# A fused decoder layer on one core: a third score bank, transforms folded in half, and shared-expert steps moved behind the last expert blocks

## The reference

```python
x = _layernorm(x + attn(x))        # 16 heads of 8, 4 key heads, rms norm and rope on q and k,
                                   # scores 50*tanh(s/50), causal softmax
x = _layernorm(x + xattn(x, ctx))  # cross attention to 32 context rows gives c_t; then
    x = layernorm(x_text) * (1 + mod_gate * scale_in) + mod_gate * shift_in      # scales from c_t
    Kf = jnp.fft.rfft(K, n=2 * L, axis=-1)             # K: kernel of a 64-state recurrence, 512 taps
    xf = jnp.fft.rfft(x, n=2 * L, axis=1)
    y = jnp.fft.irfft(xf * Kf.T[None], n=2 * L, axis=1)[:, :L] + x * D_skip
    xt = x_text + y * (1 + mod_gate * scale_out) + mod_gate * shift_out
    return layernorm(xt + gelu(layernorm(xt) @ W1 + b1) @ W2 + b2)
x = _layernorm(x + ffn(x))         # mean of 2 shared experts of width 512, plus the top 2 of 8
                                   # routed experts of width 512, weighted by a softmax of the gates
```

## Time and profile before

| | |
|---|---|
| median of 3 runs | 561.07 us (558.0 to 561.37) |
| profiled execution | 563.88 us, its span 562.1 us |
| granted TensorE clock, mean | 0.904 |
| PE busy | 443.5 us (79%) |
| DVE busy | 330.3 us (59%) |
| ACT busy | 328.2 us (58%) |
| POOL busy | 247.3 us (44%) |
| DMA | 51.53 MB, mean 92 GB/s |

### The profile page before, as it was taken

How to read it: one execution, slowest core, us unless ns; L and a number is a source line. 1 busy time by engine, 2 the same in 40 slices (tenths; PEclk the granted TensorE clock), 3 DMA queues, 4 the chain that set the end, 5 groups by cost and what they waited for, 6 DMA issues and landing times.

```text
span 562.1 us, 9639 instructions
## 1 busy us (share of the span) xinstructions
PE 443.5 (79%) x3343; PEld 316.1 (56%) x3361; DVE 330.3 (59%) x983; ACT 328.2 (58%) x567; POOL 247.3 (44%) x306
## 2 busy tenths in 40 slices
PE   4656667378988879788798999999979699989830
PEld 3322323145657633567346865787778666878830
DVE  7877968847876565866754775546245310334214
ACT  4279769997775888877896152215536343445410
POOL 3513264423561565614446244864283574044341
PEclk9856656679999999999999999999998899999985
DMA  3788300002101000000000200165485516769831
GB/s 94 267 181 152 100 2 1 0 2 58 77 1 77 20 2 0 2 1 1 2 0 1 76 2 19 40 179 194 138 260 160 163 54 182 261 208 279 271 104 37
DMA packets 39920, 51.53 MB, mean 92 GB/s; under 512 B 8769, under 2 KB 29025, under 8 KB 39873
## 3 DMA queue, kind: packets, MB, share of 16 engines
q1 hardware_dynamic: 37376, 45.78, 28.1%
q0 software_dynamic: 2496, 5.15, 2.6%
HBM read 41.25 MB, written 13.86 MB: 98 GB/s over the span
## 4 chain that ended last, share of the span: by engine, by line
PE 47%; ACT 22%; DVE 9%; issue 8%; POOL 8%; DMA 5%; another core or an unknown queue 1%; POOLq 0%; SPq 0%; ACTq 0%; DVEq 0%
ACT probs L1082 8%; PE ring_s L957 5%; ACT probs L1088 5%; PE bank_o L987 4%; PE bank_o L775 4%; PE bank_d L865 3%; DMA token_pairs<-y_blk,x_blk 3%; PE ring_s L760 3%; PE bank_o L973 3%; PE ring_s L951 3%; POOL expert_rows L1302 3%; PE ring_u L852 3%; PE bank_d L894 2%; PE ring_u L844 2%; PE bank_r L641 2%
## 5 line engine op out<-in xcount | busy, mean ns | idle before, releaser
L1082 ACT ACTIVATE probs<-ring_s 128x512 f32<-128x512 f32 (+1 forms) x192 | 92.3, 524 | 39.2 <-PE ring_s L760 19.5
L760 PE MATMUL ring_s<-qT,kT 128*128 128x128 bf16 (+3 forms) x238 | 62.5, 330 | 41.6 <-ACT probs L1082 31.3
L1254 POOL TENSOR_SCALAR_AFFINE_SELECT probs<-probs 128x256 f32<-128x256 f32 (+1 forms) x96 | 50.6, 558 | 100.1 <-ACT probs L1088 100.1
L1135 ACT ACTIVATE g_ring<-ring_s,w_blk 128x128 f32<-128x128 f32 x184 | 52.3, 371 | 47.5 <-PE ring_s L957 47.5
L1088 ACT ACTIVATE probs<-probs 128x2560 f32<-128x2560 f32 x32 | 74.4, 2335 | 1.1
L1311 POOL DMA_INDIRECT token_pairs<-y_blk,x_blk x46 | 44.6, 970 | 66.2 <-DVE y_blk L1838 59.9
L760 PEld LDWEIGHTS ring_s<-qT,kT 128*128 128x128 bf16 x256 | 20.8, 100 | 80.2 <-ACT probs L1082 61.0
L957 PE MATMUL ring_s<-xT_blk,w_blk 128*128 128x128 f32 x368 | 51.1, 284 | 5.9 <-DVE xT_blk L1831 3.9
L1188 POOL TENSOR_TENSOR rstd<-var_eps,neg_half 128x4 f32<-128x4 f32 x24 | 25.0, 1040 | 67.4 <-DVE var_eps L1507 67.4
L957 PEld LDWEIGHTS ring_s<-xT_blk,w_blk 128*128 128x128 f32 x368 | 46.5, 198 | 7.9 <-ACT g_ring L1135 4.3
L775 PE MATMUL bank_o<-probs,vv 128*32 128x128 f32 (+3 forms) x512 | 43.2, 483 | 3.7 <-POOL probs L1254 3.6
(11 more groups left out here) (365 smaller groups left out, 932.3 us busy)
## 6 DMA issues: line engine op xcount, KB each, us to landing
w_blk<-expert_pack SPq DMA_DIRECT2D x46, 514.0 KB, 5.0
expert_pack<-in_L_ffn_W SPq DMA_DIRECT2D x16, 256.0 KB, 8.9
expert_rows<-blank SPq DMA_DIRECT2D x6, 520.0 KB, 3.6
x_blk<-expert_rows SPq DMA_DIRECT2D x10, 260.0 KB, 4.4
y_pair<-token_pairs SPq DMA_DIRECT2D x4, 512.0 KB, 4.9
x_in<-in_x SPq DMA_DIRECT2D x4, 256.0 KB, 2.9
cosm<-in_c_cos SPq DMA_DIRECT2D x1, 1024.0 KB, 5.9
sin_fwd<-in_c_sin_fwd SPq DMA_DIRECT2D x1, 1024.0 KB, 8.8
```

The source lines that it names most:

```text
L760: last = mm(bank[:, c:c + w], kT[:, r, p // 2, P * j:P * (j + 1)], qT[:, p, P * j:SEQ], start=True, stop=True)
L1082: f(probs[:, pair % PAIRS_HELD, BASE[n]:BASE[n] + WIDTH[n]], ring_s[k % 2][:, 0:WIDTH[n]], ACT.Tanh, scale=1.0 / (CAP * float(np.sqrt(np.f ...
L1135: last = f(g_ring[:, s % RING, P * n:P * (n + 1)], ring_s[s % 2][:, P * n:P * (n + 1)], ACT.Gelu, bias=w_blk[:, k % SLOTS, HID + n:HID + n ...
L1254: last = g.affine_select(out=v, in_=v, compare_op=ALU.is_ge, fill=0.0, base=0, pattern=[[0, v.shape[1]], [1, P]], channel_multiplier=-1)
```

## The change

- **Score banks.** `ring_s` has three banks; the third is what was `bank_m`. A head pair takes five fills of 512 columns, since the last two of 256 share one. `rows`, `yT` and the vectors go to `bank_o`, and PV waits until the tokens of the PV before it have been read there. The block transposes use `ring_s[2]`.
- **Folded transforms.** Frequencies are sorted into even and odd, and samples into sums and differences with their mirror image, so that a step of `dft` or `conv` has two matmuls in place of four. New are `mirror` (two matmuls with a matrix that reverses rows), `fold` on DVE, `unfold` on DVE (three instructions) and `back` (two matmuls); `shape_out` is in two instructions. The kernel is transformed the same way (`kmirror`, `kfold`). The tables are half as wide and shifted by half a step, which DVE computes at the start (`halves`, some 25 instructions on 128x4, and four times `half`, four instructions on 128x256); the forward tables are made by 16 transposes (`tab`) and four copies on ACT. `spectra` has 17 instructions in place of 3.
- **Units.** The last six shared units of batch 3 come behind the last block, as units 72 to 77; group 1's blocks are 49 to 71. The downs of these blocks alternate between `bank_d` and `ring_u[0]`, so that the sum of batch 3 can stay in `bank_o`.
- **Buffers and SP.** Six `y_blk` in place of three, four slots of `g_ring` in place of three. SP issues a group's first six weight loads ahead of the wait for the scatters.
- **New lists** for all four engines.

```diff
-FILLS = [(r, tiles) for tiles in ([(0, 0)], [(1, 0), (3, 384)], [(2, 0)]) for r in range(2)]
+FILLS = [[(r, j, c) for j, c in tiles] for tiles in ([(0, 0)], [(1, 0), (3, 384)]) for r in range(2)] + [[(0, 2, 0), (1, 2, 256)]]
+BANKS = 3
-RING = 3
+RING = 4
-YS = 3
+YS = 6
+LATE = 6
+UNITS = shared_units(0) + shared_units(1) + block_units(0) + shared_units(2) + shared_units(3)[:-LATE] + block_units(1) + shared_units(3)[-LATE:]
 PE_ORDER = steps("""
-    xT.0 qkv.0 fold1 fold2 fold3 fold4 vectors qT.0.0 qT.0.1 qT.0.2 qT.0.3 qT.0.4 s.0.0.0 s.0.0.1 s.0.0.2 s.0.0.3
+    xT.0 qkv.0 fold1 fold2 fold3 fold4 vectors pack qT.0.0 qT.0.1 qT.0.2 qT.0.3 qT.0.4 qT.0.5 s.0.0.0 s.0.0.1 s.0.0.2
...
 ACT_ORDER = steps("""
-    xT.0 qkv.0 functions fold1 fold2 fold3 qT.0.0 qT.0.2 qT.0.4 s.0.0.0 s.0.0.1 s.0.0.2 s.0.0.3 s.0.0.4 s.0.0.5
+    functions xT.0 qkv.0 fold1 fold2 fold3 qT.0.0 qT.0.2 qT.0.4 s.0.0.0 s.0.0.1 s.0.0.2 s.0.0.3 s.0.0.4 s.0.1.0
...
+            def turn_over(dst, src, at):
+                for j in range(NJ):
+                    last = mm(dst[:, P * j:P * (j + 1)], flip[:, :], src[:, at + NJ - 1 - j, :], start=True, stop=True)
+                return last
+
+            def half_dft(f, c, src):
+                at = 0 if (f == 0) == (c < NJ) else NJ
+                for j in range(NJ):
+                    last = mm(ring_u[f][:, P * c:P * (c + 1)], (cos_fwd, sin_fwd)[f][:, j, P * c:P * (c + 1)], src[:, at + j, :],
+                              start=(j == 0), stop=(j == NJ - 1))
+                return last
...
             def values(quad):
                 b, q = divmod(quad, NQUAD)
                 pe.wait_ge(masked, 2 * quad + 2)
-                if quad >= 1:
-                    pe.wait_ge(oT_ready, quad)
+                if quad == 0:
+                    pe.wait_ge(b1_ready, 1)
+                else:
+                    pe.wait_ge(y_ready, quad)
...
+            def mirror(b):
+                pe.wait_ge(xmod_ready, b + 1)
+                turn_over(ring_u[0], xn, NJ).then_inc(mirror_ps, 1)
...
+            def back(b):
+                pe.wait_ge(unfolded, b + 1)
+                turn_over(bank_d, unrolled, NJ).then_inc(back_ps, 1)
...
+            def unfold(b):
+                dve.wait_ge(conv_ps, b + 1)
+                sym, anti = (bank_d[:, HALF * k:HALF * (k + 1)].rearrange("p (j d) -> p j d", j=NJ) for k in range(2))
+                one(v.tensor_copy(unrolled[:, 0:NJ, :], anti))
+                one(tt(unrolled[:, NJ:NT, :], sym, unrolled[:, 0:NJ, :], ALU.subtract))
+                tt(unrolled[:, 0:NJ, :], sym, unrolled[:, 0:NJ, :], ALU.add).then_inc(unfolded, 1)
...
             for g in range(GROUPS):
                 sp.wait_ge(table_ready, g + 1)
+                for q in range(SLOTS):
+                    load_block(g * NB + q)
+                if g:
+                    sent(g - 1)
+                    load_pair(GB * (g - 1))
                 sp.wait_ge(scattered[g], 16 * 2 * NT * GB)
```

488 lines of the change are left out of this document (285 added, 203 removed).

## The result

The changed kernel takes 552.5 us (median of 4 runs, 551.69 to 552.84) against 560.9 us before; the ratio is 0.9859, 95% interval 0.9829 to 0.9889. That is 8.4 us, where 30 were forecast. In the profiled executions the last norm ends at 545.22 us in place of 556.21, 11.0 us sooner (the profiled execution of before was 3 us above its median, that of after at its median). Every ratio here leaves out executions over 1.5% above the fastest of their kernel, while the medians hold all.

What follows compares the result with a forecast made beforehand. PE was taken to bound about 128 to 539 us, DVE the first 34, the tail its own chain. 562.1 + 11 - 24.9 - 3 + 6 - 6 - 6 + 4.3 - 11.5 = 532.0, against the median 531 us; range 512 to 554.

Steps and rivals of the forecast that it cites:

- Folded transforms, -24.9 and -3: PE's transforms: 28 fewer matmuls a batch save 24.9 us over four batches; the kernel's own transform saves about 3.
- The start, +11: Up to the first tanh: new ACT and DVE work delays it 17.3 us, partly given back in ACT's idle time; net +11.
- New waits, +6: In the batches' transforms: PE waits for DVE's fold, unfold and halved shape_out, costing 6 us (bounds 0 and 12).
- Third bank, -6: From 128 to 345 us: PE's 9.9 us of waits for ACT to leave a score bank shrink, saving 6 us.
- Buffers, -6: In the expert blocks: six y_blk and four gelu slots remove DVE's scatter waits and PE's idle time, saving 6 us.
- Readiness, +4.3: At both groups' starts: PE arrives before the rows are loaded, costing 3 us for group 0 and 1.3 for group 1.
- Tail, -11.5: After the last block's down: shared units run beside the closing chain, so down and end come 11.5 us sooner.
- B: Whole kernel: start +17, folding's waits 12, readiness 8 and ring -3 eat the savings; 550 us, chance 0.16.
- C: PE's clock falls behind the added exchanges, four falls of 2.5 us each; 541 us, chance 0.05.
- E: Up to 345 us DVE becomes the bound, folding there brings nothing, start stays +17; slower at 574 us, chance 0.06.

## Why the prediction was wrong

The sign and the range were right; the size was not (30 us forecast, 8.4 measured). Of the 21.6 us that are missing the table has 5.9 at the 16th exp, 10.1 between it and the first scatter, and 3.1 behind that (the rest is the profile of before against its median).

- **Folded transforms, -24.9 and -3: the step that failed.** It said that "all four lie where PE sets the pace: batches 0 to 2 in the 217 us at 88%". A busy share of 88% isn't a bound. In the old lists, where I had read that row, the halved matmuls gave 0.9 us of the 18.7 that lie there, at most about 6.5 with the clock held up (estimate), and the changed kernel as a whole gained 10.1 in that stretch where I had 20.2. What took the saving there were waits of PE for ACT, POOL and DVE (32.6 us idle in place of 22.3) and, behind them, the lower clock. Doubling the matmuls in the new lists cost in full, so a busy row can be a bound from one side only. How the 10.1 divides among folding, third bank and new lists stays open: no run has the new lists with one of them alone. Batch 3's share, behind the attention, is in the 16.7 us that PE's busy time fell there.
- **The start, +11: the give-back was the error.** Undoing order and tables gave back 13.6 us at the 16th exp. The first tanh was 13.6 late; I had 17.3 with 8.8 coming back in ACT's idle time. Nothing came back, and the tables took the place of what could have: DVE is the busiest engine up to 117 us (96.5 us against ACT's 73.3) and had got them there. That I left the constants of the recurrence out of the path ahead of `squares` did no harm only because the fold ended at the same time. The -3 for the kernel's transform isn't seen in that stretch either.
- **New waits, +6:** 3.0 us for unfold and spectrum in the middle stretch; the other waits for DVE there (rank, x1T) were not in my list. **Third bank, -6:** 4.7 us of ring waits went there; what that is worth in time is open, since no run has two banks with the new lists.
- **Buffers, -6:** 4 on the old lists, 10.6 as the new lists use them.
- **Readiness, +4.3:** the first block transposes of both groups start without a wait, at 375.64 and 473.15; PE idles 1.0 us ahead of group 1. It is about +1.
- **Tail, -11.5:** mechanism right, 9.8 by the run without late units, and PE works 9.8 us behind the last block's down. The term added up lengths that overlap on PE: it took 1.02 + 1.05 for a unit, where units follow each other in 1.75.
- **Rivals.** B (the savings are eaten) comes nearest by its number, 550, but that is luck: its waits were 12 (3.0 measured) and its readiness 8 (1). C is not settled: the clock does fall, and where it was held up in the changed kernel that gave under 1 us, but in the old lists single falls cost 1.6 and 3.8 us. Against C the prediction named waits of up to 0.8 us at a clock of 1.00, which is one row; the longest in that stretch was 2.2. E, that folding brings nothing before 345 us, fits the old lists as far as they were run, but put it on DVE alone and kept the start at +17; DVE's cut alone gave 2.4 us (ratio 0.994).

What stays open: which order of the lists would let the front's saved work show. The kernel with its start undone shows that about 9 us lie there (ratio 0.970 against 0.986, from two sessions), but it has no shifted tables, and the one try to make them elsewhere (POOL) lost 5 us. And whether the old lists would use halved matmuls at a clock held up.

## What to carry to other kernels

Don't price a cut by an engine's busy share: halve the work in question in the old kernel first, outputs aside; one run tells whether the schedule can use it as it is. Look at the granted clock in that run before reading a null result: new waits can lower it and hide part of the gain. A delay that can be undone without effect on the events may still be real: undo the other candidates with it, since two delays side by side hide each other. Where a change has parts in different stretches, cut both traces at common events and graft the parts onto the old kernel one by one; here the small part at the end was worth all of the gain.
